# A decoder layer on one core: cross-attention scores from split queries and keys, and the first norm on another engine

## The reference

```python
def reference(x, ctx_1024, mask, ...):
    x = _layernorm(x + _L0_attn_ref(x, WQ, WK, WV, WO))          # causal, 16 heads of 16
    x = _layernorm(x + _L0_xattn_ref(x, ctx_1024, ctx_1024, mask, Wq, bq, Wk, bk, Wv, bv, Wo, bo))
    x = _layernorm(x + _L0_ffn_ref(x, ...))                      # 16 experts, top 4, and a shared one
    return x

def _L0_xattn_ref(queries, keys, values, mask, Wq, bq, Wk, bk, Wv, bv, Wo, bo):
    q = split_heads(queries @ Wq + bq)
    k = split_heads(keys @ Wk + bk)
    v = split_heads(values @ Wv + bv)
    scores = jnp.einsum('bhqd,bhkd->bhqk', q, k) / jnp.sqrt(HD)  # 16 heads, 64 keys
    scores = jnp.where(mask, -1e15, scores)
    attn = jax.nn.softmax(scores, axis=-1)
    ctx = jnp.einsum('bhqk,bhkd->bhqd', attn, v)
    return merge_heads(ctx) @ Wo + bo

def _layernorm(x, eps=1e-05):
    m, v = jnp.mean(x, axis=-1, keepdims=True), jnp.var(x, axis=-1, keepdims=True)
    return (x - m) / jnp.sqrt(v + eps)
```

## Time and profile before

| | |
|---|---|
| median of the timed runs | 653.34 us |
| span of the profiled execution | 708.7 us |
| TensorE busy in it | 612.1 us, 86% |
| VectorE | 469.8 us, 66% |
| ScalarE | 351.4 us, 50% |
| GpSimd | 317.3 us, 45% |
| mean granted TensorE clock | 0.948 |
| share of the chain that ended last, score matmuls L1675 | 4% |

### The profile page before, as it was taken

The page is one execution under the profiler, slowest core; times in us unless marked ns, Lnnn a source line. Parts: engine busy times, 40 slices in busy tenths (PEclk is TensorE's granted clock), DMA queues, the critical chain, the costliest instruction groups (busy, mean ns, idle before and its releaser), DMA issues.

```text
span 708.7 us, 12877 instructions
## 1 busy us (share of the span) xinstructions
PE 612.1 (86%) x3830; PEld 369.6 (52%) x3830; DVE 469.8 (66%) x1303; ACT 351.4 (50%) x734; POOL 317.3 (45%) x393
## 2 busy tenths in 40 slices
PE   6878999999999999898799997959743899889885
PEld 3434434434443343254457765746443788877752
DVE  0369788788787886039658783825442766767687
ACT  1312266666766667734555542423131555556544
POOL 8413313233442432444875336362745455555550
PEclk9989899999999999999999998788985999999999
DMA  5767776146263400009400002120344675548847
GB/s 166 170 169 151 146 226 93 43 68 89 38 93 58 53 19 18 19 16 350 157 1 1 1 27 95 33 97 32 113 141 124 190 207 180 155 147 285 275 173 237
DMA packets 52673, 82.51 MB, mean 116 GB/s; under 512 B 11984, under 2 KB 29648, under 8 KB 52304
## 3 DMA queue, kind: packets, MB, share of 16 engines
q1 hardware_dynamic: 45744, 62.26, 35.7%
q0 software_dynamic: 6864, 19.44, 7.5%
HBM read 53.38 MB, written 32.48 MB: 121 GB/s over the span
## 4 chain that ended last, share of the span: by engine, by line
PE 64%; DVE 15%; issue 5%; another core or an unknown queue 4%; DMA 4%; ACT 4%; POOL 3%; SPq 1%; POOLq 0%; ACTq 0%; DVEq 0%
PE ps L1512 9%; PE ps L1488 9%; PE ps L1777 9%; PE ps L1471 8%; DVE neg_max L947 5%; PE ps L1800 5%; PE ps L1675 4%; PE ps L1694 3%; PE ps L1756 2%; PE ps L1789 2%; PE ps L1684 2%; PE ps L1476 2%; PE ps L1620 2%; PE ps L1711 2%
## 5 line engine op out<-in xcount | busy, mean ns | idle before, releaser
L947 DVE TENSOR_REDUCE neg_max<-ps 128x1 f32<-128x512 f32 (+3 forms) x304 | 182.1, 654 | 45.0 <-PE ps L1476 28.1
L791 ACT ACTIVATE temps<-ps 128x1024 f32<-128x1024 f32 (+1 forms) x192 | 147.6, 812 | 81.5 <-PE ps L1488 81.5
L690 POOL TENSOR_SCALAR_AFFINE_SELECT temps<-temps 128x256 f32<-128x256 f32 x128 | 52.2, 411 | 151.8 <-ACT temps L791 150.8
L1471 PE MATMUL ps<-stacks 96*128 96x512 bf16 (+3 forms) x384 | 106.8, 336 | 11.1 <-DMA stacks<-qk_parts 5.2
L761 POOL DMA_INDIRECT expert_outputs<-x_T,w_o_xqkv x79 | 77.4, 980 | 69.2 <-ACT x_T L911 40.5
L1488 PE MATMUL ps<-stacks 99*128 99x512 bf16 (+3 forms) x384 | 95.3, 334 | 3.3 <-DMA stacks<-m_rows 1.7
L1512 PE MATMUL ps<-temps,v_group 128*32 128x512 f32 (+3 forms) x768 | 82.7, 502 | 1.7 <-ACT temps L791 0.9
L1777 PE MATMUL ps<-w_split,block_x 128*128 x474 | 73.3, 292 | 6.3 <-issue 3.3
L754 POOL DMA_INDIRECT expert_slots<-x_tok,w_o_xqkv x64 | 62.3, 974 | 28.7 <-issue 17.2
L1777 PEld LDWEIGHTS ps<-w_split,block_x 128*128 128x128 f32 x474 | 64.3, 196 | 8.3 <-issue 8.1
L1488 PEld LDWEIGHTS ps<-stacks 99*128 99x128 bf16 x384 | 27.5, 99 | 77.1 <-ACT temps L791 50.9
(11 more groups left out here) (219 smaller groups left out, 1089.7 us busy)
## 6 DMA issues: line engine op xcount, KB each, us to landing
stacks<-qk_parts SPq DMA_DIRECT2D x96, 128.0 KB, 5.8
v_group<-expert_slots SPq DMA_DIRECT2D x79, 138.5 KB
qk_parts<-temps SPq DMA_DIRECT2D x8, 768.0 KB, 4.4
w_raw<-in_w SPq DMA_DIRECT2D x4, 1024.0 KB, 10.2
early_parts<-expert_outputs SPq DMA_DIRECT2D x4, 1024.0 KB
expert_slots<-in_pad SPq DMA_DIRECT2D x16, 138.5 KB
expert_slots<-in_pad SPq DMA_DIRECT2D x1, 2077.5 KB
x_T<-in_xT SPq DMA_DIRECT2D x4, 512.0 KB, 7.0
```

The costliest lines, as they stand in the source:

```text
L690: nc.gpsimd.affine_select(diag, diag, [[0, 2], [1, P]], ALU.is_ge, zero, base=0, channel_multiplier=-1).then_inc(b_cut, 1)
L791: nc.scalar.activation(pt[:, n % 4, :, 0:w], ps[:, 2 + 2 * (n % 2):4 + 2 * (n % 2), 0:w], ACT.Exp, scale=SCALE).then_inc(b_exp, 1)
L947: nc.vector.tensor_reduce(nmx[:, c, h0:h0 + nh, i], ps[:, A_BANKS[n % 3], 0:w * nh].rearrange("p (h k) -> p h k", h=nh), axis=AX.X, op=ALU ...
L1471: last = nc.tensor.matmul(ps[:, A_BANKS[n % 3], w * s:w * s + w], qs[0:KR, ua, h0 + s, P * i:P * i + P], ks[0:KR, ua, h0 + s, CH * c:CH * ...
```

## The change

It has three parts. In the score step S one fp32 matmul becomes three fp32r matmuls of 512 columns into the same PSUM buffer: high part of the queries with high part of the keys, high queries with low keys, low queries with high keys (`PASSES`). `q2` becomes a pair of fp32r buffers and `kbd` gets a high and a low copy.

Who makes the parts: ScalarE's move of the queries (L830, now L847) writes the high part, rounded to fp32r. VectorE makes the low part from PSUM plus bias less the high part (`low_queries`), for a group of four tiles each at tiles 8, 12 and 16 of its loop and after it. ScalarE makes the high part of the keys in two copies of 1024 columns, one per batch element, at tile 14 of its loop (L853); GpSimd subtracts for the low part after its loop over the tiles. The first S, and a projection that reuses a PSUM buffer, wait for the low queries (`xq_low`) where they waited for `xq_kept`; the first S also waits for `xk_low`.

The first norm is applied as the second one is: VectorE's 128x256 operation becomes a 128x1 one (`norm_shift`), and ScalarE applies (`apply_norm`), tile t + 1 between the weight split of its step t and the copy of the transposes of tile t.

```diff
         pool:
+            for b in range(B):
+                pool.wait_ge(xk_high, b + 1)
+                nc.gpsimd.tensor_tensor(k_low[:, :, b], kbd[:, :, b].rearrange("p o h k -> p o (h k)"), k_high[b][:],
+                                        ALU.subtract).then_inc(xk_low, 1)
             pool.wait_ge(xq_ready, 8)
...
         act:
+            def apply_norm(n, t):
+
+                act.wait_ge(ln_shift, n + 1)
+                nc.scalar.activation(x[:, t, :], x[:, t, :], ACT.Identity, bias=nmr[:, t % 4:t % 4 + 1],
+                                     scale=rstd[:, t % 4:t % 4 + 1]).then_inc(ln_done, 1)
+
+            apply_norm(0, 0)
             for t in range(NT + 1):
                 if W_TILE <= t < NT:
                     w_high(t - W_TILE)
+                if t + 1 < NT:
+                    apply_norm(t + 1, t + 1)
                 if t < NT:
                     act.wait_ge(xT_ready, t + 1)
...
-                        nc.scalar.activation(q2[:, o, CH * (t // 4 - 1):CH * (t // 4)], ps[:, 6 + o, :],
+                        nc.scalar.activation(q2[0][:, o, CH * (t // 4 - 1):CH * (t // 4)], ps[:, 6 + o, :],
                                              ACT.Identity, bias=bq[:, o:o + 1]).then_inc(xq_kept, 1)
+                if t == KV_TILES[1] - 1:
+                    act.wait_ge(kv_kept, 16)
+                    act.wait_ge(o_scaled, NG)
+                    for b in range(B):
+                        nc.scalar.activation(k_high[b][:], kbd[:, :, b].rearrange("p o h k -> p o (h k)"),
+                                             ACT.Copy).then_inc(xk_high, 1)
...
         dve:
-            def norm_apply(n, t, slot):
+            def low_queries(c):
+
+                dve.wait_ge(xq_ready, 2 * c + 2)
+                for o in range(2):
+                    dve.wait_ge(xq_kept, 2 * c + o + 1)
+                    nc.vector.scalar_tensor_tensor(q2[1][:, o, CH * c:CH * c + CH], ps[:, 6 + o, :], bq[:, o:o + 1],
+                                                   q2[0][:, o, CH * c:CH * c + CH], ALU.add, ALU.subtract)\
+                      .then_inc(xq_low, 1)
+
+            def norm_shift(n, slot):
                 dve.wait_ge(ln_pow, n + 1)
-                nc.vector.tensor_scalar(x[:, t, :], x[:, t, :], mv[:, slot, 0:1], rstd[:, slot:slot + 1],
-                                        ALU.subtract, ALU.mult).then_inc(ln_done, 1)
+                nc.vector.scalar_tensor_tensor(nmr[:, slot:slot + 1], mv[:, slot, 0:1], -1.0, rstd[:, slot:slot + 1],
+                                               ALU.mult, ALU.mult).then_inc(ln_shift, 1)
...
                 if t >= 1:
-                    norm_apply(t - 1, t - 1, (t - 1) % 4)
+                    norm_shift(t - 1, (t - 1) % 4)
+                if t >= 8 and t % 4 == 0:
+                    low_queries(t // 4 - 2)
+            low_queries(NT // 4 - 1)
...
         pe:
-                            pe.wait_ge(xq_kept, s // 4 * 2 + o - 1)
+                            pe.wait_ge(xq_low, s // 4 * 2 + o - 1)
...
-            pe.wait_ge(xq_kept, 8)
+            pe.wait_ge(xq_low, 8)
+            pe.wait_ge(xk_low, B)
...
-                    nc.tensor.matmul(ps[:, n % 2, :], q2[:, o, P * t:P * t + P],
-                                     kbd[:, o, t // TB].rearrange("p h k -> p (h k)"), start=True, stop=False)
+                    for i, (qp, kp) in enumerate(PASSES):
+                        keys = k_low[:, o, t // TB, :] if kp else k_high[t // TB][:, o, :]
+                        nc.tensor.matmul(ps[:, n % 2, :], q2[qp][:, o, P * t:P * t + P], keys, start=(i == 0), stop=False)
```

20 lines of the change are left out of this document (9 added, 11 removed).

## The result

The changed kernel takes 658.5 us (median of 22 runs) where the kernel before, in the same rounds, took 653.3 (22 runs). The ratio is 1.0068 with a 95% interval of 1.0044 to 1.0092: 4.4 us slower, 2.9 to 6.0. The forecast was 650.2 with a range up to 654.5. Executions fall into a faster and a slower state: the ratios, and the medians and mean clocks from here on, are of the faster runs alone, and the profiled execution of the changed kernel (664.6 us) is one of two slower ones among its 22.

A forecast was written before the change was run, and what follows sets the result against it. The prediction took TensorE to bound the score loop, with the first norm's VectorE and GpSimd in lockstep ahead of it. 5.6 us saved on scores less 2.5 us for a later first score took 653.3 to 650.2 us, range 645.5 to 654.5.

The forecast's parts named there:

- The score's price: Score loop: three fp32r passes take 0.66 us in place of 0.86, each score 0.20 us shorter (0.15 to 0.215).
- What of it arrives: Score loop: the saving counts where TensorE is the bound, 28 of 32 scores, 5.6 us (3.6 to 6.9).
- the stretch from 366 to 402: Score loop: 36 us in which TensorE is busy for 36.00 and VectorE 28.08, so TensorE is the bound.
- The later first score: End of first norm: the first score starts 2.5 us later, 1.8 from ScalarE's late copy plus 0.7 from low parts.
- the copy of tile 15: ScalarE's queue at the end of the first norm: last copy of transposes at 353.3 in place of 351.5, 1.8 us late.
- the waits for the second half projections: ScalarE in the first norm: twice it sits out the second half of a query projection, about 1.2 us each time.
- The projection was kept as it was: Last query projection: stays at 5.39 us, since TensorE stands idle about as long before it as it did.
- The last low parts: Last group's query low parts: VectorE takes 0.69 us and a 0.05 hop serially before the first score, 0.7 us.
- The hold on VectorE: First norm: VectorE's 128x1 operation is still held until GpSimd's running operation ends, on a shorter operation.
- The keys' low parts: GpSimd ahead of the first score: 2.36 us each, over at about 356, so hidden.
- The slip eats the gain: Rival, end of first norm: first score 5.3 us late with more waiting and a half-clock projection; 653.0, no change; 18%.
- ScalarE paces every tile: Rival, first norm: each tile costs 3.3 us instead of 2.50 through ScalarE's waits; 3.9 us slower, 657.2; 9%.

The follow-up runs named there:

- e2: Changed kernel with the first norm back on VectorE, so only the scores and the parts they need change: 660.4 us, ratio 1.0125 to the kernel before.
- e3: Changed kernel with the two copies of the keys' high parts on VectorE in place of ScalarE: 656.4 us, ratio 1.0072 to the kernel before.
- e0: Kernel before, unchanged, run again for a second profile and as a measure of the comparison itself: 653.1 us, ratio 1.0005.
- e8: Changed kernel with 27 idle matmuls at the end of the first norm and 49 in and behind the score loop: 653.8 us, ratio 1.0014.
- e5: Changed kernel with one score pass of three, the low parts left out: 658.8 us, ratio 1.0065 to the kernel before.
- e11: Changed kernel with one score pass of three and all the idle matmuls, 27 and 49: 651.3 us, ratio 0.9973 to the kernel before.
- e12: Changed kernel with two scatters per step of the score loop in place of three: 651.6 us, ratio 0.9999 to the kernel before.
- e15: Kernel before with two scatters per step and idle matmuls, 15 ahead of the loop and 49 in and behind it: 650.8 us, ratio 0.9956.
- e4: Changed kernel with 27 idle matmuls in TensorE's gaps at the end of the first norm: 654.7 us, ratio 1.0019 to the kernel before.
- e9: Kernel before with 15 idle matmuls at the end of the first norm: 653.4 us, ratio 0.9996.
- e13: Changed kernel with two scatters per step and all idle matmuls, 27 ahead of the loop and 49 in and behind it: 649.0 us, ratio 0.9939.
- e16: Changed kernel with two scatters per step, keys' high parts on VectorE, and idle matmuls, 21 ahead of the loop and 49 in and behind it: 651.3 us, ratio 0.9947.
- e1: Kernel before with only the first norm moved to ScalarE, scores still one fp32 matmul: 652.0 us, ratio 0.9976.
- e10: Kernel before with 15 idle matmuls ahead of the score loop and 49 in and behind it: 652.8 us, ratio 0.9998.

## Why the prediction was wrong

**The score's price** held at its lower bound: 0.15 us per score, not 0.20, a pass 0.233 us, three passes and the mask 0.92 (0.86 to 0.90 foreseen). The Trainium skill, "TensorE: Matmul & The Clock Gate", section "Back-to-back issue gap", gives 216 ns for a lone pass of this size; in this kernel's loop the trace has 8% more.

**What of it arrives** is the step that failed. The prediction said that the saving counts where TensorE is the bound, gave up the four scores ahead of the first routing wait, and kept 28. It should have asked what holds behind that wait. From the first routing on a tile takes 8.15 us on GpSimd whenever six scatters stand ahead of a power, and the groups follow each other in e2 and e3 as in e0 (27.1 and 30.1 us from the second on). So the 11 scores that start behind the first scatter bought nothing. The lead of the 21 ahead (21 x 0.15 = 3.2, of which 1.3 came through at the first scatter) was gone at the next group, where the clock had fallen (0.57 in e3); with idle matmuls in the loop (e8) 2.1 came through and stayed. Of 5.6 us predicted, none arrived: 297 us from the first score to the end in e2 and e3 as in e0. That something other than the scores sets the loop's time is shown by e5 and e11, where two of three passes are left out; that it is GpSimd's queue is read from the chain and borne out by the second spacing of e12 to e15, not by the first. The prediction took the stretch from 366 to 402 for the whole loop; the scatters begin at 417.8 in that trace.

**The later first score** was foreseen in kind and undersized: 2.5 us forecast, 5.2 measured behind the load. By terms: the copy of tile 15 came 2.7 us later (1.8 forecast), with the norms, the key copies and the waits for the second half projections as described (gaps of 0.88, 1.03, 0.16 and 1.03 in the trace; the norm of one tile waited 0.80, of another 0.22). The projection was kept as it was, "since TensorE stands idle about as long before it as it did". That step was wrong: the waits ahead of it were 1.87, 1.15 and 2.57 us in place of 0.18, 2.04 and 0.76, and it took 1.5 us more, most of it at the lower clock; e4 and e9 together put the clock's share at 1.5 to 2.5 us of the stage's loss. The last low parts took 1.0 us more and not 0.7: VectorE makes both behind the second half, since their buffer lies over the transposes that this half still reads. In the times of the first profile the first score stands at 363 to 364, where about 360 was forecast and 363 was named as the limit.

**The hold on VectorE** was right. The 128x1 operation took 1.22 us beside GpSimd's subtraction and ended with it (342.69 and 342.67), and 0.15 without, as the Trainium skill, "SBUF — State Buffer", section "SBUF: two separate sides", has it. The keys' low parts were hidden, as forecast.

**The rivals.** "The slip eats the gain" came nearest in kind, with a slip of 5.3 us and a projection 1.5 us longer; but it held a gain of 5.6 against it that did not exist. "ScalarE paces every tile" came near in number (657.2) and is not what happened, since ScalarE's gaps ahead of the norms are 0.80 and 0.22 us, not 1.25 on each tile.

**What stays open.** Whether 2 us at the first score always show in the time. They do from e2 to e3 and with the clock's help in e4; from e13 to e16 and in e9 they don't, but the intervals, 2 us and more to either side, do not exclude it. e3 and e16 each lose what they had gained by the second group, with the clock down in the first spacing (0.57 and 0.50). In the profiles with three scatters a step, the one with stalls aside, the first spacing is 28.4 us wherever the clock stays up in it (e0, e1, e4, e8, e10, e11) and 29.7 to 32.7 where it falls (the others); the runs do not tell whether that is a matter of chance in the clock. And why the first spacing does not fall with two scatters is argued from one chain, not tried.

## What to carry to other kernels

A saving on the busiest engine counts up to the next place where the chain runs through another queue. Find that place in the chain first (here the scatters ahead of a small power on GpSimd), and then count the instructions that lie ahead of it. Work that is taken from TensorE in a stretch with waits can also lower its clock and be paid back, as in e5. Ahead of the long projection here (e4, e9) cheap matmuls in the gaps cost nothing that could be measured, since TensorE waits there anyway.

## What the runs showed of the hardware

With less work TensorE's clock was lower: with one score pass of three the mean granted clock was 0.955, the lowest of all kernels (0.964 with three, in the same rounds), and with idle matmuls in the same kernel 0.974. The Trainium skill, "TensorE: Matmul & The Clock Gate", section "Part 1: The HAM clock gate", says that the gate follows how busy the engine has been; e4, e5 and e11 agree, while in e16 it fell behind 14 us of which the profile shows TensorE busy for 13.78. The clock also goes with most of the scatter between executions of one program: over 121 runs of the kernel before, the mean granted clock and the time have a correlation of -0.90, worked out from the runs' times and clocks. So a difference of a few us is better read from many runs than from one profile, and the positions in the tables above come from one profile each.
